# A state-space scan and attention on one core: queues reordered, half of the softmax sums on VectorE, scatters moved, two convolution taps shared out

## The reference

```python
x = layernorm(x + mamba(x))                    # 256 channels, 16 states, 4 convolution taps
x = layernorm(x + cross_attention(x, ctx))     # 16 heads of 8, rope, causal and padding mask
x = layernorm(x + moe(x))                      # 8 experts, 2 chosen per token, 512 hidden
# mamba
xs, res = split(x @ W_in)
u = silu(causal_conv(xs, conv_w) + conv_b)     # 4 taps per channel
delta = softplus(u @ W_x[:, :64] @ W_dt + b_dt)
h[t] = exp(delta[t] * A) * h[t-1] + delta[t] * B[t] * u[t]     # per channel and state
y = (sum_n h[:, n] * C[:, n] + u * D) * silu(res)
out = y @ W_out
```

## Time and profile before

| | us |
|---|---|
| median of three runs | 1009.97 |
| profiled execution | 999.74 |
| its span, first to last instruction | 997.8 |
| TensorE busy | 872.5 (87%) |
| VectorE busy | 742.2 (74%) |
| ScalarE busy | 719.8 (72%) |
| GpSimd busy | 581.1 (58%) |

### The profile page before, as it was taken

One profiled execution on the slowest core, in us unless ns is written; L12 is line 12 of the kernel. 1 busy time (PEld: TensorE's weight loads), 2 busy tenths in 40 slices (PEclk: granted clock), 3 DMA queues, 4 the chain that ended last, 5 costly groups with the idle time before them and its releaser, 6 DMA issues.

```text
span 997.8 us, 29713 instructions
## 1 busy us (share of the span) xinstructions
PE 872.5 (87%) x10285; PEld 580.5 (58%) x10286; DVE 742.2 (74%) x1503; ACT 719.8 (72%) x2213; POOL 581.1 (58%) x394
## 2 busy tenths in 40 slices
PE   5578988989899798889989888988898999999996
PEld 2234554454455345445544544554588999999972
DVE  2589788878878977887897797788764666666657
ACT  3597997898799689879959985965924555555556
POOL 2588359629846973984797398397152333333331
PEclk8799999999999999999999998999999999999999
DMA  3435101500610240061033006004041111111135
GB/s 106 107 66 142 41 4 48 123 16 11 151 42 14 71 112 18 9 156 37 14 86 86 19 8 154 8 13 175 7 136 52 48 48 48 48 48 46 47 118 169
DMA packets 68476, 66.12 MB, mean 66 GB/s; under 512 B 9040, under 2 KB 62480, under 8 KB 67984
## 3 DMA queue, kind: packets, MB, share of 16 engines
q1 hardware_dynamic: 63440, 55.58, 21.5%
q0 software_dynamic: 4352, 8.99, 2.7%
q10 hardware_dynamic: 576, 0.10, 0.1%
HBM read 48.51 MB, written 16.13 MB: 65 GB/s over the span
## 4 chain that ended last, share of the span: by engine, by line
PE 44%; ACT 21%; DVE 18%; issue 12%; POOL 3%; DMA 2%; SPq 0%; DVEq 0%; POOLq 0%; ACTq 0%
ACT prob L714 8%; PE pair_b L1746 7%; PE pair_a L1742 7%; DVE prob L967 6%; ACT decays L673 5%; DVE hst L967 4%; PE pair_b L1538 3%; PE bank L1754 3%; PE y_ps L1754 3%; PE bank L1549 3%; DVE u L933 2%; PE pair_a L1570 2%; PE pair_a L1478 2%; PE y_ps L1538 1%; PE pair_a L1436 1%
## 5 line engine op out<-in xcount | busy, mean ns | idle before, releaser
L673 ACT ACTIVATE decays<-w,a_neg 128x256 f32<-128x256 f32 x512 | 218.7, 509 | 47.1 <-DVE prob L967 30.1
L496 POOL TENSOR_TENSOR hst<-hst,c_rep 128x1024 f32<-128x1024 f32 x64 | 151.3, 2372 | 12.6 <-DVE hst L967 12.0
L576 POOL DMA_INDIRECT y<-aoT,dest x72 | 77.3, 1074 | 135.1 <-DVE aoT L1289 131.5
L496 POOL TENSOR_TENSOR prob<-prob,c_rep 128x1024 f32<-128x1024 f32 x56 | 132.1, 2368 | 9.4 <-DVE prob L967 8.9
L528 POOL DMA_INDIRECT xg<-x_all,pos x64 | 64.9, 1014 | 88.4 <-DVE pos L1117 77.1
L714 ACT ACTIVATE prob<-pair_b,nmax 128x128 f32<-128x128 f32 x256 | 90.2, 399 | 2.1 <-DVE nmax L1025 2.1
L967 DVE TENSOR_TENSOR_SCAN prob<-decays,pair_b 128x1024 f32<-128x1024 f32 x32 | 72.8, 2276 | 24.0 <-issue 18.6
L714 ACT ACTIVATE prob<-y_ps,nmax 128x128 f32<-128x128 f32 x256 | 90.6, 413 | 0.0
L1436 PE MATMUL pair_a<-w,du_tok 64*32 64x256 f32 x1792 | 63.4, 392 | 29.8 <-DVE prob L967 15.1
L1436 PE MATMUL pair_b<-w,du_tok 64*32 64x256 f32 x2048 | 71.6, 389 | 19.5 <-DVE prob L967 12.1
L488 POOL TENSOR_TENSOR w<-diag,b_tok 128x1024 f32<-128x1024 f32 x32 | 61.9, 1959 | 37.5 <-ACT b_tok L654 23.5
(11 more groups left out here) (291 smaller groups left out, 2194.6 us busy)
## 6 DMA issues: line engine op xcount, KB each, us to landing
w<-d_dram SPq DMA_DIRECT2D x64, 256.0 KB, 6.5
c_rep<-c_dram SPq DMA_DIRECT2D x64, 128.0 KB, 3.8
qk<-xg SPq DMA_DIRECT2D x79, 65.0 KB
d_dram<-zpos SPq DMA_DIRECT2D x8, 512.0 KB, 3.2
xn<-in_x SPq DMA_DIRECT2D x8, 256.0 KB, 2.9
cn<-in_ctx SPq DMA_DIRECT2D x8, 256.0 KB, 3.1
mask_b<-in_mask SPq DMA_DIRECT2D x8, 256.0 KB, 3.3
w<-in_w1T SPq DMA_DIRECT2D x1, 2048.0 KB, 7.8
```

Source lines behind the costliest of these rows:

```text
L496: g_.tensor_tensor(by_state(ring(k)), by_state(ring(k)), c_rep[:, :, toks[r]].rearrange("p q (i t) -> p i q t", i=2), ALU.mult).then_inc(s ...
L576: pool.indirect_dma_start(y2[:, :], bass.IndirectOffsetOnAxis(ap=dest[:, b:b + 1], axis=0), ys[:, b % 4, :], None).then_inc(s[f"y_out{b % ...
L673: last = A(by_state(decays[:, k % 3, :])[:, :, q, :], delta_rep[:, b, toks[r]].rearrange("p (i t) -> p i t", i=2), ACT.Exp, scale=a_neg[:, ...
```

## The change

Four things are done, all in the passes.

On TensorE the first y sum goes behind the entries of step 7, columns of B and convolution products two steps or one later; the last y sum goes ahead of a transpose group, and in the first tile of attention keys, transposes and queries stand later, the second half of the scores earlier. VectorE's and ScalarE's orders follow: ScalarE runs the silus of u before its copies of the keys, and the silu of the gate behind them.

For t = 1 to 3 the exponentials of the first eight heads no longer use the accumulator; VectorE sums these 8 x 128 values per row in one reduction (`sums_of_exps`), queued one tile ahead, behind its last copy of the tile before.

GpSimd's scatters all stand in the attention half: one after the first diagonals, four before the query add, one after it, and one more after each of the next two operations.

Of the second channel half, VectorE adds only the tap at distance 1. ScalarE copies bank 6 twice, scaled by the other two taps, into `rotk` (`later_taps`), and GpSimd adds the two copies, shifted by 2 and 3 tokens, to u (`taps_later`).

```diff
+            def taps_later(c):
+                for i in range(2):
+                    at(pool, "conv_raw_sb", 2 * (c - 2) + i + 1)
+                    at(pool, "taps_sb", 6 * c + 4 + i)
+                    o = u[:, c % 2, 1, :].rearrange("p (s t) -> p s t", s=S)[:, :, 2 + i:]
+                    g_.tensor_tensor(o, o, rotk[:, i, :].rearrange("p (s t) -> p s t", s=S)[:, :, 0:L - 2 - i], ALU.add).then_inc(s["taps_sb"], 1)
             def add_q(g, r):
...
                 for k in range(NU - 1):
-                    if m >= 2 and k < S:
-                        scatter(m - 2, (k,))
                     times_c(m, k)
+                    if c is not None and k == 10:
+                        taps_later(c)
                     if e is not None:
...
                 if m >= 2:
-                    scatter(m - 2, (S,))
+                    scatter(m - 2, (0,))
                 if e is not None:
...
                 if m >= 2:
-                    scatter(m - 2, (S + 1,))
+                    scatter(m - 2, (1, 2, 3, 4))
                 add_q(m, 1)
                 if m >= 2:
-                    scatter(m - 2, (S + 2,))
+                    scatter(m - 2, (5,))
                 add_bo(m)
                 if m >= 2:
-                    scatter(m - 2, (S + 3,))
+                    scatter(m - 2, (6,))
                 if e is not None:
                     add_k(e)
+                if m >= 2:
+                    scatter(m - 2, (7,))
+                if e is not None:
                     masked(e)
...
+            def later_taps(c):
+                at(act, "conv_ps", 2 * c + 2)
+                at(act, "k_sb", c - 1)
+                for i in range(2):
+                    A(rotk[:, i, :], bank[6], ACT.Copy, scale=taps[:, 1, 1 - i:2 - i]).then_inc(s["conv_raw_sb"], 1)
             def res_out(c, h):
...
-            def silus(c):
+            def silus_u(c):
                 nc.scalar.preload_act_table_set("silu_and_others")
...
                     u_silu(c, h)
+            def silus_res(c):
                 at(act, "res_sb", 2 * (c - 2) + 2)
...
                         at(act, "s_neg", 16 * g + 4 * t + c + 1)
-                    last = A(prob[:, t % 2, c, j, :], bank[2 + c][:, j * L:(j + 1) * L], ACT.Exp, bias=nmax[:, t % 2, h:h + 1],
-                             accum_out=den[:, t % 2, h:h + 1])
+                    mine = {} if t and not k else {"accum_out": den[:, t % 2, h:h + 1]}
+                    last = A(prob[:, t % 2, c, j, :], bank[2 + c][:, j * L:(j + 1) * L], ACT.Exp, bias=nmax[:, t % 2, h:h + 1], **mine)
                     if j == 3:
...
                             x2_in(w)
-                    if c is not None and k == 5:
+                    if c is not None and k == 4:
                         x_in(c, 6)
...
                     if c is not None:
-                        if k == 6:
+                        if k == 7:
                             conv_out(c, 0)
-                        if k == 9:
+                        if k == 10:
+                            later_taps(c)
                             conv_out(c, 1)
...
                     res_out(c, 1)
+                    silus_u(c)
                 x1_in(g, 0)
...
                 if c is not None:
-                    silus(c)
+                    silus_res(c)
+                exps(g, 0, 0)
                 if e is not None:
                     duT_out(e, 1, 6)
-                exps(g, 0, 0)
+                exps(g, 0, 1)
                 ln_scale1(g, 1)
-                exps(g, 0, 1)
-                x1_in(g, 1)
                 for t in range(S):
...
                         exps(g, t + 1, 0)
+                    if t == 0:
+                        x1_in(g, 1)
                     pT_out(g, t, 2)
...
+            def sums_of_exps(g, t):
+                at(dve, "p_sb", 16 * g + 4 * t + 2)
+                at(dve, "rden_sb", S * g + t - 1)
+                v_.tensor_reduce(out=den[:, t % 2, 0:H // 2], in_=prob[:, t % 2, 0:2].rearrange("p c j m -> p (c j) m"), axis=AX.X,
+                                 op=ALU.add).then_inc(s["den_sb"], 1)
             def inverses(g, t):
                 at(dve, "p_sb", 16 * g + 4 * t + 4)
+                if t:
+                    at(dve, "den_sb", (S - 1) * g + t)
                 v_.reciprocal(rden[:, t % 2, :], den[:, t % 2, :]).then_inc(s["rden_sb"], 1)
...
                             second_norm(w)
-                    if c is not None and k == 7:
+                    if c is not None and k == 8:
                         taps_in(c, 0, 6, (2, 1, 0))
-                    if c is not None and k == 9:
-                        taps_in(c, 1, 6, (2, 1))
                     if k == 10:
...
                         if c is not None:
-                            taps_in(c, 1, 6, (0,))
+                            taps_in(c, 1, 6, (2,))
                     if k == 12:
...
                     best(w)
-                first_norm(g, 1)
-                if w is not None:
-                    which(w)
                 for t in range(S):
...
                         maxima(g, t + 1, 0)
-                    if t == 0 and e is not None:
-                        rope_k(e, 0, 0)
+                    if t == 0:
+                        first_norm(g, 1)
+                        pT_out(g, t, 1)
+                        if w is not None:
+                            which(w)
+                        if e is not None:
+                            rope_k(e, 0, 0)
                     inverses(g, t)
...
                         normed(g, t - 1)
-                    pT_out(g, t, 1)
-                    if t == 0:
-                        rope_q(g, 1)
+                    if t:
+                        pT_out(g, t, 1)
                     if t == 1 and w is not None:
...
                         mark(w)
-                    if t == 0 and e is not None:
-                        rope_k(e, 1, 0)
                     if t + 1 < S:
...
                         states(e, 0)
+                    if t == 0:
+                        rope_q(g, 1)
                     pT_out(g, t, 3)
+                    if t == 0 and e is not None:
+                        rope_k(e, 1, 0)
+                    if t + 1 < S:
+                        sums_of_exps(g, t + 1)
                 if w is not None:
...
                 if c >= 2:
-                    at(pe, "taps_sb", 6 * c + 6)
+                    at(pe, "taps_sb", 6 * c + 4)
+                    at(pe, "conv_raw_sb", 2 * (c - 2) + 2)
                     at(pe, "res_sb", 2 * (c - 2) + h)
...
                         y_begin(m, k - 4)
-                    if k == 5:
+                    if k == 6:
                         y_add(m, 0)
...
                             step(e, 1, 5)
-                        if k == 6:
+                        if k == 7:
                             b_columns(e, 7)
...
                     if c is not None:
-                        if k == 5:
+                        if k == 7:
                             conv(c, 0, 6)
-                        if k == 8:
+                        if k == 9:
                             conv(c, 1, 6)
-                        if k in (11, 13):
-                            res(c, (k - 11) // 2, 6)
+                        if k in (12, 13):
+                            res(c, k - 12, 6)
                     if k == 11:
...
                 scores(g, 0, 0)
+                y_add(g, 3)
                 if e is not None:
                     du_t(e, 1, 6)
-                y_add(g, 3)
+                scores(g, 0, 1)
                 residual(g, 1)
-                scores(g, 0, 1)
                 first_out(g, 1)
...
                         scores(g, t + 1, 0)
-                    if t == 0:
-                        if e is not None:
-                            keys(e, 0, 0)
-                        x1_t(g, 1)
                     if t:
...
                     if t == 0:
-                        queries(g, 1)
                         if e is not None:
-                            keys(e, 1, 0)
+                            keys(e, 0, 0)
+                        x1_t(g, 1)
                     if t + 1 < S:
...
                     head_t(g, t, 2)
+                    if t == 0:
+                        if e is not None:
+                            keys(e, 1, 0)
+                        queries(g, 1)
                     if t == S - 1 and e is not None:
```

More of the change, by code:

```diff
@@ L219, in build @@
         names = """passed w_load w_later w13_load w2_load pool_const dve_const act_const
-        x_load0 x_load1 x_load2 ctx_load mask_load xT_ps xT_sb conv_ps conv_sb taps_sb res_ps res_sb u_sb sres_sb sres_direct
+        x_load0 x_load1 x_load2 ctx_load mask_load xT_ps xT_sb conv_ps conv_sb conv_raw_sb taps_sb res_ps res_sb u_sb sres_sb sres_direct
         dtl_ps dtl_sb z_ps z_sb zexp_sb softp delta_sb du_sb delta_set c_sb btok_ps btok_sb duT_ps duT_sb bdiag_sb
@@ L223, in build @@
```

(2 more changed lines are left out.)

## The result

The changed kernel takes 1016.86 us (median of 6 runs, 1014.07 to 1019.12) where the kernel before took 1008.75 beside it (6 runs, 1008.28 to 1010.68): 1.0081 of before, 95% interval 1.0063 to 1.0099. It is slower by 8 us; the forecast was 20.6 us faster. The time lies outside the range of 978 to 1003 us.

The account below looks back on a forecast made before the run. No engine is full; different engines bound different stretches, so only waits on the path give time. Passes save 6 x 2.4 + 3.5 + 2.7 = 20.6 us, 1009.97 to 989.4 us; range 978 to 1003 us.

Parts of the forecast that it names:

- GpSimd's scatters: Scan half: four scatters of 1.2 us each leave GpSimd's front, paying for its two added taps and hardly more.
- the port step: End of scan: VectorE's two-SBUF-input add and GpSimd's last product share one read interface; the first to start keeps it.
- The port at the end of the scan: VectorE's add and GpSimd's last product overlap; the last y sum starts 1.7 us earlier, not the scans' 3.1.
- the move of the taps: Scan half: VectorE drops two taps, 1.45 us, with 0.6 us back waiting for ScalarE's copy; GpSimd gains 2.5 us.
- The wait before the eighth scan: Scan half: moving the first y sum saves 2.9 us there; 0.5 us comes back before the ninth scan, 2.4 us saved.
- The sums: Attention: half the exponentials without accumulator, VectorE reductions of 1.2 us; a tile goes from 6.78 to 6.30, 1.0 us saved.
- The first tile: Attention: last y sum to the third tile's scores takes 15.3 us for 14.86, leaving 1.3 us saved.
- the scatters in a row: Attention: GpSimd's scatters before the query add end at 281, the add is asked for at 282.5; hidden, 1.5 us spare.
- the rival in which GpSimd is too late for those scores: Third tile's scores: scatters take 2.4 us each, six passes 2.1 us worse, about 1018 us; 8 in 100.
- attention gives nothing: Rival: VectorE's reduction delays the maxima, tiles stay at 6.78 us; about 1001 us; 22 in 100.
- The port costs nothing: Rival at the scan's end: the last y sum starts at 266.0, 3.9 us a pass, 979 us; 15 in 100.

Follow-up runs that it names:

- e8: The kernel before the change, with only GpSimd's scatters moved as in the change: 1014.19 us, 1.0129 of the kernel before.
- e1: The changed kernel, with GpSimd's first product of passes 2 to 7 waiting again for VectorE's write of the positions: 991.95 us, 0.9911 of the kernel before.
- e7: The changed kernel, with GpSimd's first product again behind the positions and both taps back on VectorE: 977.07 us, 0.9759 of the kernel before.
- e3: The changed kernel, with the accumulator on all exponentials and no sums on VectorE: 1018.16 us, 1.0171 of the kernel before.
- e9: The kernel of e7, with the accumulator again on all exponentials and no sums on VectorE: 987.69 us, 0.9856 of the kernel before.
- e5: The changed kernel, with GpSimd's first product again behind the positions and the fifteenth scan's product on VectorE: 985.01 us, 0.9849 of the kernel before.
- e11: The kernel of e7, with the fifteenth scan's product on VectorE in the two passes without taps: 978.01 us, 0.9766 of the kernel before.

## Why the prediction was wrong, point by point

**The failed step: GpSimd's scatters.** The forecast wrote that the scatters taken out of GpSimd's front "thus pay for the taps and hardly more", and costed their move by GpSimd's own time and by the third tile's scores. It did not ask what else the first of them did: its wait for the positions kept the first product behind `prk`. The term is missing from the sum. It is worth 13 thousandths alone (e8) and 15 in the changed kernel (e1), some 13 to 15 us, of the 29 by which the forecast was off. Of the rest, the clock behind the held query add is 1.2 to 1.8 us in most passes, and attention gained 0.44 us a pass less than forecast; both follow below. The wait was in the kernel before and the held add in the trace; what was left undone is to use the port step's own rule on every two-input operation of VectorE that GpSimd's products could now meet, and not only on the query add.

The Trainium skill, "SBUF — State Buffer", section "Who interferes with whom", also says which VectorE work is free of this: an instruction with at most one SBUF input, outside the two-port modes. The trace agrees: the rotation out of PSUM at 263.96 takes 0.73 us for two beside GpSimd's products, as long as in e7 with GpSimd idle part of the time, and a scan, with one input in PSUM, took 2.26 us beside a product of 2.36 in the kernel before; the add right behind the rotation is held. By that rule the list to walk before a reorder starts with `prk`, the query add and the last product. It is not the whole list. A small cast with one input also ran longer beside GpSimd's add of the keys, here in e7, VectorE and then GpSimd (0.16 us in the second pass):

```profile
279.62 0.71 DVE L1119 CAST idxf<-i 128x8 f32<-128x8 uint32 x1
```

```profile
279.01 1.28 POOL L523 TENSOR_TENSOR qk<-rotk 128x512 f32<-128x512 f32 x1
```

**The port at the end of the scan: right in place and size, but the clock was missing.** The forecast put the start of the last y sum at 50.05 us of the pass; e1, where the start of the scan is repaired, has it at 49.83. GpSimd's last product ends at 50.1 in the changed kernel, 48.3 without the 1.8 from the start (forecast 48.45), and the taps take 1.16 each (1.25). (The forecast's 265.9 for that end is 0.16 above its own terms, 235.04 + 30.7.) What was missed, and is the second term that the sum lacks: TensorE idles for 2.1 us in that hold, its clock falls in most passes, and the work behind is then 1.2 to 1.8 us longer (35.17 to 35.81 us from the last y sum to the next pass in the second to fourth, sixth and seventh pass of e1, 34.01 in the fifth). Before, it idled 0.48 there, and the clock was at 1.00 over the whole pass. With the clock, the taps on GpSimd cost 15 thousandths (e7 against e1). The forecast had counted the move of the taps as part of a gain.

**One pass, added up.** The pass from 216.46 is 87.2 us; the forecast for it was 83.6. The last y sum starts 1.9 us later than foreseen (51.98 for 50.05), nearly all of it the hold of `prk`, and from there to the next pass it is 35.20 us for 33.57. Of these 1.63 us the clock is 1.19, since with the clock up the same stretch takes 34.01 (e7). The other 0.44 is gain that attention didn't bring: it was 34.30 before, so 0.29 was gained there and not 0.73. In the three passes behind it the clock falls at the start as well, and the fourth scan is 1.7 to 2.0 us later again.

**The wait before the eighth scan: right.** It is gone, with 0.60 us before the ninth (forecast 0.5) and 0.80 before the tap (0.6). VectorE of the changed kernel:

```profile
237.99 2.29 DVE L990 TENSOR_TENSOR_SCAN prob<-decays,pair_b 128x1024 f32<-128x1024 f32 x1
240.87 2.29 DVE L990 TENSOR_TENSOR_SCAN hst<-decays,pair_a 128x1024 f32<-128x1024 f32 x1 [0.60 <-PE pair_a L1471]
```

**The sums: right, with sizes off.** Tiles go from 6.78 to 6.30 us and VectorE's reduction takes 1.21 (1.2). Eight exponentials without accumulator save 0.74 us and not 0.4, because they are 0.25 us apart (2.01 us from the first of them to ScalarE's next instruction) and not 0.30; TensorE's 6.30 us is the bound anyway. From the third tile's scores to the next pass it brings 0.73 us (18.18 in e7, 18.91 before) where the forecast had 1.0. In time the step is worth 9 to 10 us by e3 and e9, where its share of the sum was about 7; the seven distances of e9 and e7 show 6.4 of that, and where the rest lies was not followed. ScalarE, eight without and the first with (its second row is the read of the accumulator):

```profile
288.98 2.17 ACT L735 ACTIVATE prob<-pair_b,nmax 128x128 f32<-128x128 f32 x8
...
291.49 0.40 ACT L735 ACTIVATE prob<-y_ps,nmax 128x128 f32<-128x128 f32 x1
291.74 0.24 ACT L735 ACTIVATION_READ_ACCUMULATOR prob<-y_ps,nmax 128x1 f32 x1
```

**The first tile and the scatters in a row: right.** Four follow each other 1.26 us apart and end at 282.0, in front of the add that is asked for at 284.7; the wait of TensorE for it is 0.79 us (0.7). From the last y sum to the mask in front of the third tile's scores e7 takes 14.45 us, but there the wait now stands behind the mask; to the scores themselves it is 15.83 us, before 15.39. That is 0.44 longer, as the forecast had it (15.3 for 14.86). So the rival in which GpSimd is too late for those scores did not happen. It is the one I had on the slower side, 1018 us; the time came out near it for another reason.

**The other rivals.** That attention gives nothing is refuted by e9. "The port costs nothing" (979 us, 0.969 of the median) did not happen in the changed kernel, where both held operations take 2 us. The time comes near it in e7, 0.9759, where the port is kept free at both ends by order and with the taps left out.

**What stays open.** How much of e1's 15 thousandths is the hold and how much the clock behind it was not separated by a run. By the rows, the seven distances of the changed kernel are 17.0 us longer than e1's; five holds of 1.8 us are in them, and three falls of the clock at the start of 1.7 to 2.0. What decides whether the clock falls behind equal idle times is open, and a filling of just the right length was not tried. In the profiled execution of the changed kernel the last pass and what follows up to the experts took 9 us longer than in its repetition (119.2 and 110.2 us). About half of it is one wait of ScalarE, which the profile puts down to no engine of this core; in the repetition it is 2.15 us, as in the kernel before:

```profile
750.02 0.60 ACT L757 ACTIVATE x2T<-bank 128x512 f32<-128x512 f32 x1 [6.73 <-remote]
```

What it waited for is not shown, nor whether the 9 us between the chips are the same thing. It is no part of the argument.

## What to carry to other kernels

An operation that is moved away takes its waits with it. Ask of each what it kept apart, above all an engine's small two-input instruction from GpSimd's long one: 64 columns can cost 2 us. When GpSimd is given work, look at what its last instruction meets on VectorE, and at whether TensorE stands idle meanwhile. And when a change of several parts comes out slower, undo them singly: here two moves cost more than all the others brought, and without the two it is 2.4% faster than before.

## What the runs showed of the hardware

A VectorE product of 128x64 with both inputs in SBUF took 0.21 us alone and 2.04 beside a GpSimd product of 2.38 that began 0.4 us before it. It was held to the end of that, not slowed in proportion. It happened the same way in 6 passes of every kernel in which nothing kept the two apart. Not every pair behaves like this: in the kernel before, the 128x128 product `rden_wide` at 287.50 took 0.69 us (0.29 in most tiles) beside a GpSimd tensor-scalar instruction that ran from 287.44 to 289.38, so it was not held to the end of that one.

TensorE's granted clock has two levels here, 2.4 and 1.2 GHz (1.00 and 0.50 in the windows). In the last y sums of the first seven passes of all profiled kernels without filling, e5 apart, it fell behind 28 of 33 idle stretches of 1.7 to 3.4 us and behind none of 44 of 0.5 to 1.4 us; in e5, with 0.49 and 1.17 us close together, in 4 of 7 passes; with the idle time filled by unused products in none of 14. In the eighth pass it fell behind 0.5 us in three kernels (the one before, the changed one and e11). At the start of the scan, behind the same 2.17 us of idle time, the projections took 1.9 us in 14 passes and 2.7 to 3.5 us in 16 (the third to seventh pass of the six kernels that hold `prk`). So a wait of 2 us makes a fall likely and does not settle it. A fall in the last y sum cost 1.2 to 1.8 us in e1.
